# Graph attention and a gated message layer over 8192 nodes: rows renumbered for the mask transposes, four weights made at a block's start

## The chip, the cores and the metric

One NeuronCore of a Trainium2 chip runs the whole program in one launch. The metric is the device time of that launch in microseconds (us), median of the runs shown; the profile is of one further execution, whose own time stands in the table below.

## The reference, cut to what matters

`x` is 8192 x 128 in float32, `adj` is an 8192 x 8192 matrix of zeros and ones in float32 (268 MB), and the layers are two.

```
h  = relu(layernorm(x));  Wh = h @ W;  f1 = Wh @ a1;  f2 = Wh @ a2
e  = leaky_relu(f1 + f2.T, 0.2);  scores = where(adj > 0, e, -9e15)
x1 = x + relu(softmax(scores) @ Wh)
h  = relu(layernorm(x1));  node = h @ W1
y  = einsum('nk,nkf->nf', node, einsum('nc,kcf->nkf', h, W2))
out = x1 + relu(adj @ y + node @ b)
```

The softmax weight of target i and source j is a product of exponentials of f1 and f2 and the mask, so the kernel computes each weight as `max(z_i, q_j) * mask` and sums `weight * (b_j Wh_j)` on TensorE; a 129th column gives the denominator.

## The kernel before, in words

**Numbering.** A block is 1024 nodes: 8 tiles of 128. Node `8p + t` of a block lies on partition `p` in tile `t` (the views in lines 53 to 55). The columns of `adj` go through the same numbering, because four neighbouring columns become four bytes of one 4-byte word, and the transposes work on words.

**Mask.** For each target block `ib` (8 of them) and each source block (8), SyncE loads a 1024 x 1024 piece of `adj` (4 MB) in two loads `h` (L287), one of the tiles 0 to 3 and one of the tiles 4 to 7. Each buffer `q = 2p + h` waits for `adj_cast`, that is, for ScalarE to have cast the piece before. ScalarE casts it to bytes (L507), TensorE transposes it as 32-bit words (`turn_mask`, L757): a chunk is four transposes, one per target tile, and chunk `k` takes the words `k // 2, k // 2 + 2, ...` of the 256 words in a row of 1024 bytes. So the 128 words that one transpose loads as its weights lie two words apart. ScalarE copies a chunk out (`evict`, L519) to `mt`, and stores `mt` to HBM (L626) for the second layer.

**Attention.** The loop is over `ib`, and in it over four `jg` with two half turns `p` each: one half turn is one source block, and has four steps `k`. In a step VectorE makes two weights of 128 x 1024 (`weigh`, L1008) into `p_sb` number `r = 2 * (k % 2) + b_`; TensorE transposes one chunk, then sums each weight into three PSUM banks (L824, 16 matmul instructions per weight), and tells `p_used[r]`. TensorE, in order, starts the sums of a block when ScalarE has copied out the banks of the block before (`copy_sums`, L602).

**Block's end.** While block `ib` is summed, the eight tiles of block `ib - 1` are finished, one per half turn: VectorE in steps 0, 1 and 2 (`finish_tile`: L979; L984, L989, L992, L995; L998, L1001), TensorE turns the result after the first sums of step 2 (L796) and multiplies it by the 16 matrices of `W2` in steps 2 and 3 (L789), ScalarE scales (L585) and GpSimd adds up (`fold`, L389, L392) and stores. Between the blocks, VectorE runs `end_block`: `start_weights` (before: the two weights of step 0 of the next block), then it waits for the sums copied out by ScalarE and computes the denominators (L1057, L1059, L1062). In `turn`, the variable `weighed` says which weights were made ahead. In block 0 nothing is finished, and `scale_rows` scales the value rows in step 1.

**Second layer.** `gather` (L881) multiplies the stored masks with the messages, four blocks' pairs after each other; `store_out` (L662) stores 512 KB for each block of 1024 rows.

**Start.** SyncE loads `x` in eight pieces of 512 KB (L293) between the first loads of `adj`; VectorE takes the statistics of piece `i + 1` (L912, L916) before it norms piece `i` (L927).

Of the kernel before, what the change touches and what calls it, by code (L numbers as in the profile page):

```python
# [38 lines left out]
def build(nc, x, adj, W, a1, a2, W1, W2, b, out):  # L39
    N, D = x.shape  # L40
    K = W1.shape[1]
    P = 128
    T = 8
    BLK = P * T
    NB = N // BLK
# [3 lines left out]
    IT = NB // 2  # L49
    HT = T // 2  # L50
    assert NB == T and BLK == 2 * HB and D == P

    adj_v = adj.rearrange("(i p t) n -> i p t n", p=P, t=T)
    x_v = x.rearrange("(i p t) f -> i p t f", p=P, t=T)
    out_v = out.rearrange("(i p t) f -> i p t f", p=P, t=T)

    zrow_d = nc.dram_tensor("zrow_d", [NT, P], FP32).ap()
    maskT_d = nc.dram_tensor("maskT_d", [NB, NB, P, C * BLK], U16).ap()
# [6 lines left out]
    with ctx:  # L65
# [15 lines left out]
        m8_words = nc.alloc_sbuf_tensor_at("m8_words", [P, 2, T, BLK // 4], FP32, offset=m8_at)  # L81
# [10 lines left out]
        ident = sb("ident", [P, P])  # L92
# [189 lines left out]
        @block.sync  # L282
        def _(sp):

            def load_adj(ib, jg, p, h):
                q = 2 * p + h
                sp.dma_start(adj_sb[:, q, :].rearrange("p (t n) -> p t n", n=BLK),  # L287
                             adj_v[bass.ds(ib, 1), :, h * HT:(h + 1) * HT,
                                   bass.ds((2 * jg + p) * BLK, BLK)].rearrange("i p t n -> (i p) t n"))\
                  .then_inc(adj_in[q], 16)  # L290

            for i in range(NB):
                sp.dma_start(wh[:, i * T:(i + 1) * T, :], x_v[i]).then_inc(x_in[i], 16)  # L293
                if i in (3, 5):
                    load_adj(0, 0, 0, (i - 3) // 2)
            sp.dma_start(wcat[:, 0:K * D].rearrange("c (k f) -> c k f", f=D),
                         W2.rearrange("k c f -> c k f")).then_inc(w2_in, 16)

            def turn(i, ib, jg, finish, last):
                for p in range(2):  # L300
                    for h in range(2):
                        q = 2 * p + h
                        if not (isinstance(i, int) and i == 0 and p == 0):
                            sp.wait_ge(adj_cast[q], i)
                            load_adj(ib, jg, p, h)

            attention_loop(sp, turn)


            for q in range(4):  # L310
                sp.wait_ge(adj_cast[q], NB * IT)
            for p in range(2):
                sp.wait_ge(mt_stored[p], 16 * 2 * IT)

            def load_messages(s):
                o = ORDER[s]
                sp.dma_start(msgs[:, o * T:(o + 1) * T, :, :].rearrange("p n c f -> p (n c f)").bitcast(FP32),
                             msg_d[:, o * T:(o + 1) * T, :].rearrange("p n f -> p (n f)").bitcast(FP32))\
                  .then_inc(msgs_in[s], 16)

            def load_masks(ii, s):
                q = s % 4

                if isinstance(ii, int) and s >= 4:
                    sp.wait_ge(conv_dve, dve_count(True, (s - 3) * T - 1, 1))
                    sp.wait_ge(conv_act, act_count(True, (s - 3) * T - 1, 1))
                elif not isinstance(ii, int):
                    sp.wait_ge(conv_dve, first_dve + (ii - 1) * NT + (s - 3) * T)
                    sp.sem_inc(past_sp, 1)
                    done = act_count(True, (s + 5) * T - 1, 1) if s < 4 else first_act + (s - 3) * T  # L330
                    sp.wait_ge(conv_act, (ii - 1) * NT + done)
                    sp.sem_inc(past_sp, 1)
                sp.dma_start(masks_w[:, q, :, :],
                             maskT_d[ORDER[s], bass.ds(2 * ii, 2), :, :].rearrange("i p w -> p i w"))\
                  .then_inc(masks_in[q], 16)

            def load_kept(ii):
                sp.wait_ge(out_ready, ii * 4 + 4)
                sp.dma_start(keeps[:, :, :], keep_d[:, bass.ds(2 * T * ii, 2 * T), :]).then_inc(keeps_in, 16)

            for s in range(4):
                load_masks(0, s)
            sp.wait_ge(turned, C * NB * NB)
            sp.wait_ge(kept, (ORDER[0] + 1) * T + 2)
            load_messages(0)
            for p in range(2):
                sp.wait_ge(mt_stored[p], 16 * NB * IT)
            for r in range(4):
                sp.wait_ge(p_used[r], 4 * NB * IT)
            for s in range(1, NB - 1):  # L350
                sp.wait_ge(kept, (ORDER[s] + 1) * T + 2)
                load_messages(s)
            for s in range(4, NB):
                load_masks(0, s)
            load_kept(0)
            with sp.Fori(0, NB // 2 - 1) as before:
                for s in range(NB):
                    load_masks(before + 1, s)
                sp.wait_ge(kept, NT + 2)
                load_kept(before + 1)  # L360
# [108 lines left out]
        def _(act):  # L469
# [118 lines left out]

            def load_xt(pb):
                act.wait_ge(mv_done, T * pb + 1)  # L590
                act.dma_start(xt[:, :, :], x_v[bass.ds(pb, 1)].rearrange("i p t f -> (i p) t f")).then_inc(xt_in, 16)

            def copy_sums(ib):
                if not (isinstance(ib, int) and ib == 0):
# [64 lines left out]

            def store_out(ii, h):  # L660
                act.wait_ge(out_ready, 4 * ii + 2 * h + 6)
                act.dma_start(out_v[bass.ds(2 * ii + h, 1)].rearrange("i p t f -> (i p) t f"),  # L662
                              outs[:, h * T:(h + 1) * T, :]).then_inc(out_stored, 16)

            convert(0, True, 1)
            for t in range(NT):
# [32 lines left out]
        def _(pe):  # L699
# [49 lines left out]
            def turn_mask(chunk, k, p, casts):  # L749

                if k < 2:
                    pe.wait_ge(adj_cast[2 * p + k], casts)
                if not (isinstance(chunk, int) and chunk < 2):
                    pe.wait_ge(evicted, chunk - 1)
                words = mt_ps[k % 2][:, :]
                for t in range(HT):
                    ins = pe.transpose(words[:, t * P:(t + 1) * P],  # L757
                                       m8_words[:, p, k % 2 * HT + t, k // 2:BLK // 4:2], ident[:, :])
                ins.then_inc(turned, 1)

            pe.wait_ge(hT_done, 2 * NB)
# [143 lines left out]
        def _(dve):  # L905
# [1 line left out]
            dve.sem_inc(mv_done, 1)  # L907
            dve.sem_inc(out_ready, 4)
            def statistics(i):
                dve.wait_ge(x_in[i], 16)  # L910
                for n in range(T * i, T * (i + 1)):
                    ins = dve.bn_stats(stat8[:, n, :], wh[:, n, :])  # L912
                ins.then_inc(stats8, 1)
                dve.wait_ge(stats8, i + 1)
                for n in range(T * i, T * (i + 1)):
                    ins = dve.bn_aggr(mv8[:, n, :], stat8[:, n, :])  # L916
                ins.then_inc(mv8_done, 1)
# [86 lines left out]
            def weigh(n, i, ib, p, k, b_, tile):  # L1004

                r = 2 * (k % 2) + b_
                dve.wait_ge(p_used[r], 4 * i + 2 * p + k // 2)
                dve.scalar_tensor_tensor(p_sb[:, r, :], zbf[:, bass.ds((ib % 2) * BLK, BLK)],  # L1008
                                         qcol[:, bass.ds(tile + b_, 1)], mtb[:, p, k // 2, :, 2 * (k % 2) + b_],
                                         ALU.max, ALU.mult).then_inc(p_ready, 1)  # L1010

            def turn(i, ib, jg, finish, last):
                for p in range(2):
                    n = 2 * i + p
                    u = i - IT
                    for k in range(C):
                        tile = (2 * jg + p) * T + 2 * k
                        dve.wait_ge(evicted, C * n + 2 * (k // 2) + 2)

                        weighed = p == 0 and k == 0 and isinstance(jg, int) and jg == 0  # L1020
                        if not weighed:
                            weigh(n, i, ib, p, k, 0, tile)
                        if finish and k < 3:
                            finish_tile(k, p, u, 2 * u + p, 2 * jg + p, ib - 1)
                        if not weighed:
                            weigh(n, i, ib, p, k, 1, tile)
                        if not finish and k == 1 and not (ends_block(jg) and p == 1):
                            scale_rows(n + 1)

            def start_weights(ib):  # L1030

                if isinstance(ib, int) and ib == 0:
                    dve.wait_ge(z0_copied, 2)
                else:
                    dve.wait_ge(zb_in, 16 * ib)
                dve.wait_ge(evicted, C * NB * ib + 2)
                for b_ in range(2):
                    weigh(NB * ib, IT * ib, ib, 0, 0, b_, 0)

            def convert(ii, first, t):  # L1040
                s, r = t // T, t % 2
# [95 lines left out]
```

## Time and profile before

| what | value |
|---|---|
| median of 3 runs | 1836.14 us (1834.46 to 1836.53) |
| profiled execution | 1837.21 us, span from first to last instruction 1835.6 us |
| granted TensorE clock, mean | 0.996 |
| TensorE matmul busy | 1807.8 us (98%) |
| weight load busy | 1580.7 us (86%) |
| VectorE busy | 1159.3 us (63%) |
| ScalarE busy | 1328.2 us (72%) |
| GpSimd busy | 634.4 us (35%) |
| DMA | 452.16 MB, mean 246 GB/s |

Busy time of matmuls overlaps, because they are pipelined; what a matmul costs is the distance from its start to the next one's start. "Idle before" is idle time of the engine just ahead of a group of instructions, and behind the arrow stands what ended it.

### The profile page before, as it was taken

How to read it: one execution, taken by the hardware profiler on the slowest of the kernel's cores; microseconds unless marked ns; L12 is line 12 of the kernel's file. 1: busy time of each engine (PE TensorE's matmuls, PEld its weight loads, DVE VectorE, ACT ScalarE, POOL GpSimd, SP SyncE). 2: the span in 40 equal slices, each digit the busy share in tenths (PEclk: the TensorE clock that was granted, in tenths of full speed). 3: DMA queues.
4: the chain of work that ended last, by engine and by line, in shares of the span. 5: the costliest groups of instructions: out<-in, count | busy, mean ns of one | idle time of the engine just before them, and what ended most of it. 6: DMA issues, size and time to landing. Idle time of an engine off the chain costs nothing.

```text
span 1835.6 us, 36204 instructions
## 1 busy us (share of the span) xinstructions
PE 1807.8 (98%) x12320; PEld 1580.7 (86%) x12320; DVE 1159.3 (63%) x1519; ACT 1328.2 (72%) x2145; POOL 634.4 (35%) x522
## 2 busy tenths in 40 slices
PE   8999999999999999999999999999999999999998
PEld 5899989889988988998898889889877788888886
DVE  7666667766766776676667667767665543443434
ACT  6866888788788788887888887788456555555554
POOL 0000255445544554554455445455554400000000
PEclk9999999999999999999999999999999999999999
DMA  9798867776777677678767767772933344445430
GB/s 330 281 354 317 329 254 278 295 290 246 294 296 268 265 299 292 247 285 297 280 252 302 289 260 271 293 288 105 393 127 140 147 161 184 145 182 199 154 143 23
DMA packets 105808, 452.16 MB, mean 246 GB/s; under 512 B 6737, under 2 KB 15137, under 8 KB 87969
## 3 DMA queue, kind: packets, MB, share of 16 engines
q1 hardware_dynamic: 86720, 356.53, 51.9%
q10 hardware_dynamic: 12208, 75.62, 10.1%
q0 software_dynamic: 6832, 19.41, 3.0%
q8 instruction: 27, 0.44, 0.1%
q14 instruction: 21, 0.16, 0.0%
HBM read 364.46 MB, written 87.07 MB: 246 GB/s over the span
## 4 chain that ended last, share of the span: by engine, by line
PE 90%; DVE 4%; ACT 2%; issue 1%; DMA 1%; POOL 0%; DVEq 0%; ACTq 0%; SPq 0%; POOLq 0%
PE ot_ps L824 47%; PE ot_ps L881 12%; PE mt_ps L881 12%; PE hw_ps L789 11%; PE mt_ps L757 6%; PE h_ps L784 1%; DVE p_sb L927 1%; DVE att L984 1%; ACT wh_mask L507 1%; ACT prod L585 1%; DVE p_sb L912 1%; DVE p_sb L1008 0%; DMA wh_mask<-in_x_dram 0%; DVE keep L989 0%; PE h_ps L796 0%
## 5 line engine op out<-in xcount | busy, mean ns | idle before, releaser
L824 PE MATMUL ot_ps<-wh_mask,p_sb 128*128 (+1 forms) x8192 | 964.3, 275 | 7.7 <-DVE p_sb L1008 7.7
L824 PEld LDWEIGHTS ot_ps<-wh_mask,p_sb 128*128 128x128 f32 x8192 | 942.5, 192 | 9.4 <-DVE p_sb L1008 8.9
L1008 DVE SCALAR_TENSOR_TENSOR p_sb<-zb,qcol,mt 128x1024 f32<-128x1024 uint8 (+1 forms) x512 | 730.6, 1455 | 246.6 <-PE ot_ps L824 172.2
L389 POOL TENSOR_TENSOR prod<-prod 128x1024 f32<-128x1024 f32 (+2 forms) x192 | 336.8, 1754 | 571.3 <-ACT prod L585 560.9
L507 ACT ACTIVATE wh_mask<-adj_sb 128x2048 uint8<-128x2048 f32 x256 | 493.5, 1932 | 1.0 <-ACT mt L519 1.0
L612 ACT ACTIVATE mask<-adj_sb 128x1024 fp32r<-128x1024 uint8 x240 | 255.5, 1065 | 173.5 <-PE ot_ps L881 173.4
L1047 DVE CAST mask<-adj_sb 128x1024 fp32r<-128x1024 uint8 x272 | 203.8, 756 | 244.4 <-PE mt_ps L881 242.9
L519 ACT ACTIVATE mt<-mt_ps 128x1024 uint16<-128x1024 uint16 x256 | 267.9, 1047 | 124.8 <-PE mt_ps L757 124.1
L585 ACT ACTIVATE prod<-hw_ps,node 128x128 f32<-128x128 f32 x1024 | 279.1, 387 | 90.8 <-PE hw_ps L789 89.8
L881 PE MATMUL mt_ps<-mask,msgs 128*128 128x512 f32 x1024 | 282.3, 397 | 1.9 <-DVE mask L1047 1.0
L881 PE MATMUL ot_ps<-mask,msgs 128*128 128x512 f32 x1024 | 274.8, 390 | 0.7
L789 PE MATMUL hw_ps<-wcat,hT 128*128 128x512 f32 x512 | 240.7, 592 | 0.0
L881 PEld LDWEIGHTS mt_ps<-mask,msgs 128*128 128x128 f32 x1024 | 191.0, 188 | 51.2 <-issue 13.0
L881 PEld LDWEIGHTS ot_ps<-mask,msgs 128*128 128x128 f32 x1024 | 191.6, 188 | 43.5 <-issue 3.4
L757 PEld LDWEIGHTS mt_ps<-ident,m_words 128*128 128x128 f32 x1024 | 151.1, 204 | 52.7 <-issue 52.3
L757 PE MATMUL mt_ps<-ident,m_words 128*128 128x128 f32 x1024 | 163.1, 282 | 0.3
L789 PEld LDWEIGHTS hw_ps<-wcat,hT 128*128 128x128 f32 x512 | 88.6, 190 | 61.8 <-issue 61.2
L392 POOL TENSOR_TENSOR msg<-prod 128x128 f32<-128x128 f32 x64 | 88.8, 1388 | 5.0
L406 POOL TENSOR_TENSOR msg<-msg 128x128 fp32r<-128x128 f32 x56 | 68.1, 1216 | 4.5
L417 POOL DMA_DIRECT2D zb<-zrow_d x7 | 3.8, 544 | 178.9 <-DVE p_sb L1008 119.8
L404 POOL CAST msg<-msg 128x128 fp32r<-128x128 f32 x56 | 58.9, 1052 | 9.3 <-POOL msg L392 9.3
L575 ACT ACTIVATE node<-h_ps 128x16 f32<-128x16 f32 x64 | 11.9, 186 | 60.0 <-PE h_ps L784 60.0
(110 smaller groups left out, 610.8 us busy)
## 6 DMA issues: line engine op xcount, KB each, us to landing
adj_sb<-in_adj_dram SPq DMA_DIRECT2D x128, 2048.0 KB, 8.7
maskT_d<-mt ACTq DMA_DIRECT2D x64, 1024.0 KB, 5.6
adj_sb<-maskT_d SPq DMA_DIRECT2D x32, 2048.0 KB, 7.7
keep_d<-keep POOLq DMA_DIRECT2D x64, 128.0 KB, 6.1
p_sb<-keep_d SPq DMA_DIRECT2D x4, 2048.0 KB, 12.0
msg_d<-msg POOLq DMA_DIRECT2D x56, 128.0 KB, 6.0
msgs<-msg_d SPq DMA_DIRECT2D x7, 1024.0 KB, 8.9
wh_mask<-in_x_dram SPq DMA_DIRECT2D x8, 512.0 KB, 10.1
```

The lines of the kernel that those rows point to most:

```text
L389: pool.tensor_tensor(prod[:, 0:n, :], prod[:, 0:n, :], prod[:, n:2 * n, :], ALU.add)\
L392: pool.tensor_tensor(msg32[:, :], prod[:, 0, :], prod[:, 1, :], ALU.add).then_inc(prod_read, 1)
L507: ins = act.activation(m8[:, q // 2, t:t + HT // 2, :].rearrange("p t n -> p (t n)"), adj_sb[:, q, part * (HT // 2) * BLK:(part + 1) * (HT ...
L519: act.activation(mt[:, p, k, :], mt_ps[k % 2][:, :].bitcast(U16), ACT.Copy).then_inc(evicted, 1)
L585: ins = act.activation(prod[:, head, :], hw_ps[g % 2][:, j * D:(j + 1) * D], ACT.Copy, scale=node[:, head:head + 1])
L612: act.activation(mask32[:, r, ib, :], masks[:, s % 4, ib, t % T // 4, :, t % 4], ACT.Copy)\
L757: ins = pe.transpose(words[:, t * P:(t + 1) * P], m8_words[:, p, k % 2 * HT + t, k // 2:BLK // 4:2], ident[:, :])
L789: pe.matmul(hw_ps[g % 2][:, :], hT[:, :], wcat[:, g * HB:(g + 1) * HB], start=True, stop=True)\
L824: ins = pe.matmul(ot_ps[h][:, (t - t0) * ROW:(t - t0 + 1) * ROW], p_sb[:, r, t * P:(t + 1) * P], rows, start=begin and t == t0, stop=end a ...
L881: ins = pe.matmul(acc_ps[2 * ib + h][:, :], msgs[:, ORDER[s] * T + t % T, c, :], mask32[:, r, ib, h * HB:(h + 1) * HB], start=t == 0 and c ...
L1008: dve.scalar_tensor_tensor(p_sb[:, r, :], zbf[:, bass.ds((ib % 2) * BLK, BLK)], qcol[:, bass.ds(tile + b_, 1)], mtb[:, p, k // 2, :, 2 * ( ...
L1047: dve.tensor_copy(mask32[:, r, ib, :], masks[:, s % 4, ib, t % T // 4, :, t % 4])\
```

## The change

It has two parts.

Rows and columns are renumbered: node `512h + 4p + b` of a block now lies on partition `p` in tile `4h + b`, in `adj`, `x` and the output alike. A transpose then takes words `128h` to `128h + 127`, one unbroken run. A load of `adj` takes 512 neighbouring rows; it still moves four pieces of 4 KB per partition. A load of `x` is split in two of 256 KB with two counts of its semaphore (16 loads in the place of 8); `xt` and the stores of the output move two pieces of 2 KB per partition instead of one of 4 KB.

VectorE makes the weights of steps 0 and 1 of the next block, four in all, in `start_weights`, before it computes the denominators of the old block. In the first half turn of a block it then makes none in steps 0 and 1.

```
-    adj_v = adj.rearrange("(i p t) n -> i p t n", p=P, t=T)
-    x_v = x.rearrange("(i p t) f -> i p t f", p=P, t=T)
-    out_v = out.rearrange("(i p t) f -> i p t f", p=P, t=T)
+    adj_v = adj.rearrange("(i h p b) n -> i h p b n", h=2, p=P, b=HT)
+    x_v = x.rearrange("(i h p b) f -> i p h (b f)", h=2, p=P, b=HT)
+    out_v = out.rearrange("(i h p b) f -> i p h (b f)", h=2, p=P, b=HT)
...
-                             adj_v[bass.ds(ib, 1), :, h * HT:(h + 1) * HT,
-                                   bass.ds((2 * jg + p) * BLK, BLK)].rearrange("i p t n -> (i p) t n"))\
+                             adj_v[bass.ds(ib, 1), h, :, :, bass.ds((2 * jg + p) * BLK, BLK)]
+                             .rearrange("i p b n -> (i p) b n"))\
...
-                sp.dma_start(wh[:, i * T:(i + 1) * T, :], x_v[i]).then_inc(x_in[i], 16)
+                for h in range(2):
+                    sp.dma_start(wh[:, i * T + h * HT:i * T + (h + 1) * HT, :],
+                                 x_v[i, :, h, :].rearrange("p (b f) -> p b f", f=D)).then_inc(x_in[i], 16)
...
-                act.dma_start(xt[:, :, :], x_v[bass.ds(pb, 1)].rearrange("i p t f -> (i p) t f")).then_inc(xt_in, 16)
+                act.dma_start(xt[:, :, :].rearrange("p (h b) f -> p h (b f)", h=2), x_v[bass.ds(pb, 1)].rearrange("i p h g -> (i p) h g")).then_inc(xt_in, 16)
...
-                act.dma_start(out_v[bass.ds(2 * ii + h, 1)].rearrange("i p t f -> (i p) t f"),
-                              outs[:, h * T:(h + 1) * T, :]).then_inc(out_stored, 16)
+                act.dma_start(out_v[bass.ds(2 * ii + h, 1)].rearrange("i p h g -> (i p) h g"),
+                              outs[:, h * T:(h + 1) * T, :].rearrange("p (h b) f -> p h (b f)", h=2)).then_inc(out_stored, 16)
...
-                                       m8_words[:, p, k % 2 * HT + t, k // 2:BLK // 4:2], ident[:, :])
+                                       m8_words[:, p, k % 2 * HT + t, (k // 2) * P:(k // 2 + 1) * P], ident[:, :])
...
-                dve.wait_ge(x_in[i], 16)
+                dve.wait_ge(x_in[i], 32)
...
-                        weighed = p == 0 and k == 0 and isinstance(jg, int) and jg == 0
+                        weighed = p == 0 and k < 2 and isinstance(jg, int) and jg == 0
...
-                for b_ in range(2):
-                    weigh(NB * ib, IT * ib, ib, 0, 0, b_, 0)
+                for k in range(2):
+                    for b_ in range(2):
+                        weigh(NB * ib, IT * ib, ib, 0, k, b_, 2 * k)
```

## Rows read from the trace of the kernel before

**Rows 1.** Busy time of each engine in the stretch of the attention.
```profile
core 0: us, PE busy (x) PEld busy (x) DVE busy (x) ACT busy (x) POOL busy (x), PEclk, DMA share, GB/s
52.00:1316.00 1264.00, 1254.15 (x9834) 1144.12 (x9835) 873.74 (x948) 996.09 (x1655) 561.66 (x447) 1.00 0.74 281
```

**Rows 2.** Waits of the whole trace: who for whom, us, times, longest.
```profile
PE ot_ps L824 <- DVE p_sb L1008: 7.7, 6, 1.4
```

**Rows 3.** Groups by line and shape: busy us, mean ns of one, idle before.
```profile
L757 PE MATMUL mt_ps<-ident,m_words 128*128 128x128 f32 x1024 | 163.1, 282 | 0.3
L757 PEld LDWEIGHTS mt_ps<-ident,m_words 128*128 128x128 f32 x1024 | 151.1, 204 | 52.7 <-issue 52.3 <-ACT wh_mask L507 0.3
L796 PEld LDWEIGHTS h_ps<-ident,xn 128*128 128x128 f32 x64 | 9.1, 143 | 1.2 <-DVE xn L1001 0.9
```

**Rows 4.** Timeline, chunks of four transposes and what follows: start us, us, what.
```profile
506.53 0.63 PE L757 MATMUL mt_ps<-ident,m_words 128*128 128x128 f32 x4
507.00 3.74 PE L824 MATMUL ot_ps<-wh_mask,p_sb 128*128 128x129 f32 x32
...
516.33 0.64 PE L757 MATMUL mt_ps<-ident,m_words 128*128 128x128 f32 x4
516.81 1.95 PE L824 MATMUL ot_ps<-wh_mask,p_sb 128*128 128x129 f32 x16
...
1827.29 0.60 PE L853 MATMUL ot_ps<-ident,prod 128*128 128x128 f32 x4
1827.72 0.60 PE L853 MATMUL h_ps<-ident,prod 128*128 128x128 f32 x4
```

**Rows 5.** Timeline of all engines, the boundary of two blocks at 510 us.
```profile
503.18 2.87 DVE L1008 SCALAR_TENSOR_TENSOR p_sb<-zb,qcol,mt 128x1024 f32<-128x1024 uint8 x2
...
511.84 0.17 DVE L1057 TENSOR_SCALAR empty<-ut 128x8 f32<-128x8 f32 x1 [5.78 <-ACT ut L602]
...
512.89 0.35 DVE L979 SCALAR_TENSOR_TENSOR att<-whsum,empty,ut 128x128 f32<-128x128 f32 x1 [0.44 <-DVE rden L1062]
513.21 1.28 DVE L1008 SCALAR_TENSOR_TENSOR p_sb<-zb,qcol,mt 128x1024 f32<-128x1024 uint8 x1
...
514.03 4.84 POOL L389 TENSOR_TENSOR prod<-prod 128x1024 f32<-128x1024 f32 x3 [8.49 <-ACT prod L585]
514.41 2.39 DVE L984 TENSOR_SCALAR att<-att,rden 128x128 f32<-128x128 f32 x1
...
517.00 1.22 DVE L989 TENSOR_TENSOR keep<-att,xt 128x128 f32<-128x128 f32 x1 [0.19 <-DVE att L984]
...
518.79 2.65 DVE L1008 SCALAR_TENSOR_TENSOR p_sb<-zb,qcol,mt 128x1024 f32<-128x1024 uint8 x2
...
520.09 2.05 PE L824 MATMUL ot_ps<-wh_mask,p_sb 128*128 128x129 f32 x16 [1.33 <-DVE p_sb L1008]
```

**Rows 6.** The same view, the first boundary, where GpSimd has nothing to fold.
```profile
193.96 0.28 DVE L984 TENSOR_SCALAR att<-att,rden 128x128 f32<-128x128 f32 x1
194.43 0.29 DVE L989 TENSOR_TENSOR keep<-att,xt 128x128 f32<-128x128 f32 x1 [0.19 <-DVE att L984]
...
195.62 3.74 PE L824 MATMUL ot_ps<-wh_mask,p_sb 128*128 128x129 f32 x32
```

**Rows 7.** Chain of waits at the start: start us, us, what.
```profile
0.99 0.69 SPq L293
...
1.74 8.03 DMA wh_mask<-in_x_dram
```

**Rows 8.** DMA issues: count, KB each, us from issue to landing.
```profile
adj_sb<-in_adj_dram SPq DMA_DIRECT2D x128, 2048.0 KB, 8.7
xt<-in_x_dram ACTq DMA_DIRECT2D x8, 512.0 KB, 7.1
```

**Rows 9.** Timeline, one load of `adj` and the first cast of it.
```profile
404.22 0.37 SPq L287 DMA_DIRECT2D adj_sb<-in_adj_dram  x1
...
438.38 1.90 ACT L507 ACTIVATE wh_mask<-adj_sb 128x2048 uint8<-128x2048 f32 x1
```

## The prediction

> **What bounds the kernel now.** I read the stretches first. Of the 1264 us of the attention (blocks 0 to 7) TensorE has a matmul under way for 1254.15 us, ScalarE is busy for 996.09, VectorE for 873.74, and the DMA engines for 0.74 of the time, at a granted clock of 1.00 [rows 1]. So TensorE sets the pace there, and what its instruction stream loses is time. Then the waits, for what it waits on in that stretch: only VectorE's weights, 7.7 us in 6 times [rows 2]. Six of the seven boundaries between blocks have such a wait, and nothing else in the stretch stops TensorE for as long. The rest can only fall if its own instructions come closer together, so the third view is that of the groups by shape, and the fourth the timeline, where the distance from start to start is the price. The second layer is not touched but for its stores.
>
> **Part 1, the transposes.** There are 1024 of them in 256 chunks of four. Their weight load, which reads words two apart, takes 204 ns; that of the other float32 transposes, which reads 128 words in a run, takes 143 ns (L796) [rows 3]. The load overlaps the matmul before it, so this difference is not the gain. The gain is in the distances. Behind sums, four transposes take 516.81 - 516.33 = 0.48 us to the start of the next sums, and behind a 512 column matmul 507.00 - 506.53 = 0.47 us [rows 4]. Four transposes of unbroken words take 1827.72 - 1827.29 = 0.43 us by the same reckoning [rows 4]; and from the spans, (0.64 - 0.28) / 3 = 0.12 us each against (0.60 - 0.27) / 3 = 0.11, where 0.28 and 0.27 are the lengths of one. Two decimals leave 0.03 to 0.05 us a chunk. I take 0.037, the lower half, because the first distance of a chunk behind a long matmul has its weight load hidden already. 256 x 0.037 = 9.5 us, between 256 x 0.03 = 7.7 and 256 x 0.05 = 12.8; below, a mechanism that isn't stride gives 0. All chunks but the first few lie in TensorE's unbroken stream, so all of it reaches the end. What is late next is nothing: ScalarE has 0.79 of the stretch and the DMA engines 0.74, and the stretch shrinks by under 1.5%.
>
> The Trainium skill speaks against this part. The page Advanced Engine Details and Errata, section SBUF Cachelines, says that reads keep full rate as long as two of them fall on each line of 16 bytes. Float32 words two apart do just that, so by this rule the stride is free, the transposes gain nothing, and the sum below would be 9.5 us higher; it is rival C. The trace disagrees as far as it can: 204 ns against 143.
>
> **Part 2, four weights ahead.** What happens at a boundary now: TensorE ends the old sums at 507.00 + 3.74 = 510.74 [rows 4]; VectorE has made two new weights (503.18 to 506.05) and idles 5.78 us until ScalarE has copied the sums, at 511.84 [rows 5]. Then come the denominators, the first step of finishing, the third weight at 513.21, and behind it L984, which takes 2.39 us, and L989, which takes 1.22. At the first boundary, where GpSimd folds nothing, these take 0.28 and 0.29 and TensorE goes on without a gap [rows 6]. At this one GpSimd's fold starts at 514.03, and VectorE's two end just behind the ends of its additions [rows 5]. So the fourth weight is made from 518.79, and TensorE, which could have started at about 516.81 + 16 x 0.112 = 518.60 (0.112 us from sum to sum: 3.74 less the last one's length of 0.28, over 31), starts at 520.09. That is 1.49 us, and the sums behind it take 2.05 instead of 1.95, 0.10 more [rows 4, 5]. Over six boundaries: 7.7 us of idle, and 6 x (0.16 + 0.10), since the idle is counted from the end of the last matmul, 0.16 behind the point at which the next could start: 9.3 us.
>
> After: the third weight needs the sums of buffer 2, done about 1.9 us before 510.74, the fourth those of buffer 3 at 510.74. A weight takes 1.28 us, so the third lies in idle time and the fourth ends at about 512.08. Both are there long before 516.8. The denominators wait behind the fourth and come 0.24 us later than now, the first finishing step the same, and L984 comes at about 513.7 to 513.8, because no weight lies between. That is just ahead of GpSimd's 514.03. If VectorE is first, the finishing is done by about 515. If L984 falls behind GpSimd, it ends at 516.8 and L989 at 518.2, as now, and the mean and variance at 518.8; but then the first weight of step 2 follows at once and is done at 520.1. TensorE wants it at 516.81 + 3.6 + 0.5 = 520.9 (two weights' sums, one chunk). What could be late next is the second weight of step 2: behind L998 and L1001, wanted at 522.7. With L1001 held once more by GpSimd's L392 or by the cast behind it, to 521.6, that weight comes at about 523.1, 0.4 us late. I take 0.2 us for all six together, 9.1 us gained; the bounds are 9.3 and 9.3 - 6 x 0.8 = 4.5. The first boundary gives nothing, and in block 0 the order of VectorE's work does not change: the same four weights come first either way.
>
> The wait for `p_used[3]` in `start_weights` now stands ahead of the denominators. What is queued behind it are L1057 to L1062 and the finishing; ScalarE's copies end at 511.84 anyway, 1.1 us behind that release, so only the 0.24 us counts. The loads of `zb` by GpSimd wait on weights that come no later. Without its idle time as cover, this step would cost VectorE 2.56 us a block, at six blocks 15 us.
>
> **Part 3, loads and stores of the new rows.** *adj*: 2 MB in pieces of 4 KB as before, 8.7 us to landing [rows 8]; the load issued at 404.22 is cast from 438.38 on [rows 9], so 25 us of slack hide any small difference. *x at the start*: the chain begins with the second piece, issued behind 0.69 us of the first and 8.03 us in landing [rows 7]; from there on VectorE works without a pause. Four issues now stand where two stood. No row has a 256 KB piece of 512-byte runs; at 0.69 us for double the runs, and 0.37 us for an issue with few descriptors (L287) [rows 9], I put one at about 0.5, so the second piece is all issued 4 x 0.5 - 2 x 0.7 = 0.6 us later. Bounds: 2 x 0.69 = 1.4 us on top, and 0.5 below nothing, if halves in flight land earlier. I take +0.4. The six later pieces have slack. *xt*: 7.1 us to landing [rows 8], issued some 12 us before its use; hidden. *Stores*: only the last one is bare; 16 pieces per engine instead of 8, the same bytes; +0.1 us, bounds 0 and 0.5.
>
> **Sum.** -9.5 - 9.1 + 0.4 + 0.1 = -18.1 us. Against the profiled execution, 1837.21 (span 1835.6 and 1.6 around it), that is 1819.1; the median of the runs is 1.07 lower, 1836.14, so 1818.0 is the forecast for a median. What can be told from no change here is about 0.2%, 3.7 us.
>
> **Rivals.**
> A, the forecast: both parts work, 1818.
> B, the wait moves: L984, L989 and L1001 each fall behind a GpSimd addition, and the second weight of step 2 is late by 0.4 to 0.8 us at six boundaries: 2.4 to 4.8 us less gain, 1820 to 1823. For it: the times are close (513.8 against 514.03). Against: 0.8 us of margin at the weight before.
> C, the stride is free and the 204 ns are due to something else, such as ScalarE writing the same buffer: 1818.0 + 9.5 = 1827.5. Against it: not only the load is longer, but the distance too, in the chunk at 506.53 as in that at 516.33 [rows 4].
> D, slower: `adj` comes slower. The same 4 KB pieces now lie 128 KB apart from partition to partition instead of 256 KB, and if memory serves that badly, the loads become the bound. The DMA engines are busy for 0.74 of the stretch, so it decides from 1 / 0.74 = 1.35 times the present time per piece (8.7 us becoming 11.7), less what the gain takes off. At 1.5 times, 1264 x 0.74 x 1.5 = 1403 us in the place of 1264: +139, 1975 us; at 1.4 times, +45, 1881. For it speaks only that no row shows this order; against it, pieces and bytes are the same.
> E, the change does nothing at boundaries, because the fourth weight's wait for the last sums holds VectorE until ScalarE's copy anyway and the stall goes elsewhere in full: 1818.0 + 9.1 = 1827.1. Against it: 2.56 us of weights move from behind the stall into idle time.
>
> **Chances.** A 0.72, B 0.11, C 0.07, E 0.04, D 0.03, and 0.03 for slower or level by something unseen. The range goes from 1813 (12.8 - 9.5 more from the transposes, 0.5 + 0.4 less at the start, and a microsecond between executions) to 1826: that holds A and B with the bounds of the start and stores, and leaves out C, D, E. Faster by over 0.2% is A, B, C, E: 0.94, of which I take 0.02 off for mishaps that no case names; within 0.2% 0.03; slower 0.05, D and the unseen.
>
> **What would show it.** Weight loads of L757 at about 140 ns and chunks of 0.44 us; no wait of TensorE for L1008, four weights running between 503 and 512 of that boundary, denominators 0.2 us behind the copied sums, L984 short or at least no stall behind it; landing of `adj` still near 8.7 us; the first norm of the start at most 1.4 us later. Wrong would be: L757 at 204 ns (C), a new wait of L824 for L1008 in step 2 (B), casts of ScalarE waiting for `adj` (D).

## The result and the profile after

The changed kernel takes 1817.96 us (median, 1816.49 to 1818.7, 4 runs) against 1835.52 (1834.46 to 1836.53) for the kernel before: a ratio of 0.990, 95% interval 0.9888 to 0.9911, 17.6 us less. The forecast was 1818.0 in a range of 1813 to 1826. The profiled execution took 1816.49 us, span 1814.9.

Lines from about 300 on have numbers two or three higher in the changed kernel: the transposes are L759, the sums L826, the weights L1010, the finishing L981, L986, L991, L1003, the fold L391, the second layer L883.

The stretches, from the starts of the first and last sums, of the kernel before and of the changed one (number, shortest/median/longest in ns, first to last start in us):

```profile
L824 PE MATMUL ot_ps<-wh_mask,p_sb x8192: 272/275/378, 61.1 to 1315.6; 128*128 x147, 128*128 128x129 f32 x53
L881 PE MATMUL ot_ps<-mask,msgs x1024: 387/389/472, 1318.4 to 1825.2; 128*128 128x512 f32 x171
```

```profile
L826 PE MATMUL ot_ps<-wh_mask,p_sb x8192: 272/275/377, 57.8 to 1294.3; 128*128 x147, 128*128 128x129 f32 x53
L883 PE MATMUL ot_ps<-mask,msgs x1024: 387/389/473, 1297.1 to 1804.3; 128*128 128x512 f32 x171
```

The attention went from 1254.5 to 1236.5 us, 18.0 less; the second layer stayed (506.8 and 507.2); the start is 3.3 us shorter, of which below. Of the two executions' difference of 20.7 us, the 18.0 are where the two parts work, and the start belongs to the execution, as shown below.

Groups by line and shape, the changed kernel, which answer to [rows 3], and the wait that answers to [rows 2]:

```profile
L759 PE MATMUL mt_ps<-ident,m_words 128*128 128x128 f32 x1024 | 153.4, 273 | 0.4 <-ACT mt L521 0.2 <-ACT wh_mask L509 0.2
L759 PEld LDWEIGHTS mt_ps<-ident,m_words 128*128 128x128 f32 x1024 | 123.6, 141 | 58.7 <-issue 58.3 <-ACT wh_mask L509 0.4
...
PE ot_ps L826 <- DVE p_sb L1010: 0.8, 1, 0.8
```

The weight load of a transpose fell from 204 to 141 ns, and TensorE's six waits for weights are gone; the one of 0.8 us that is left is that of the very first sums. The boundary at 510 us of [rows 5] is now at 502 us. Timeline of VectorE, TensorE and GpSimd there:

```profile
500.78 1.28 DVE L1010 SCALAR_TENSOR_TENSOR p_sb<-zb,qcol,mt 128x1024 f32<-128x1024 uint8 x1 [2.90 <-PE ot_ps L826]
502.57 1.28 DVE L1010 SCALAR_TENSOR_TENSOR p_sb<-zb,qcol,mt 128x1024 f32<-128x1024 uint8 x1 [0.50 <-PE ot_ps L826]
503.77 0.16 DVE L1060 TENSOR_SCALAR empty<-ut 128x8 f32<-128x8 f32 x1
...
505.21 0.29 DVE L986 TENSOR_SCALAR att<-att,rden 128x128 f32<-128x128 f32 x1
505.69 0.29 DVE L991 TENSOR_TENSOR keep<-att,xt 128x128 f32<-128x128 f32 x1 [0.20 <-DVE att L986]
...
506.90 2.40 DVE L1010 SCALAR_TENSOR_TENSOR p_sb<-zb,qcol,mt 128x1024 f32<-128x1024 uint8 x1 [0.25 <-ACT mt L521]
510.12 0.16 DVE L1000 RECIPROCAL rstd<-std 128x1 f32<-128x1 f32 x1 [0.83 <-ACT std L569]
...
498.79 3.74 PE L826 MATMUL ot_ps<-wh_mask,p_sb 128*128 128x129 f32 x32
...
504.52 3.74 PE L826 MATMUL ot_ps<-wh_mask,p_sb 128*128 128x129 f32 x32
508.09 0.60 PE L759 MATMUL mt_ps<-ident,m_words 128*128 128x128 f32 x4
508.53 3.74 PE L826 MATMUL ot_ps<-wh_mask,p_sb 128*128 128x129 f32 x32
512.11 0.60 PE L759 MATMUL mt_ps<-ident,m_words 128*128 128x128 f32 x4
512.54 1.95 PE L826 MATMUL ot_ps<-wh_mask,p_sb 128*128 128x129 f32 x16
...
505.83 5.42 POOL L391 TENSOR_TENSOR prod<-prod 128x1024 f32<-128x1024 f32 x3 [8.43 <-ACT prod L587]
```

The third and fourth weights lie in what was VectorE's idle time, each as soon as its buffer is free. L986 and L991 come at 505.21 and 505.69, just ahead of the fold's start at 505.83, and take 0.29 us each in the place of 2.39 and 1.22 [rows 5]. What the fold holds now is the first weight of step 2 (2.40 us in the place of 1.28), done at 509.30, 3.2 us before TensorE wants it at 512.54. TensorE has no gap, and a chunk takes 508.53 - 508.09 = 0.44 us.

### The profile page after: what moved, and what is told of

Its sections match the earlier page's. It is cut to its first block, busy times and chain, and to the rows that moved or that the text cites. A ratio compares the mean times of both kernels' runs of the same rounds, so it can differ in the third digit from the quotient of the medians.

```text
span 1814.9 us, 36206 instructions
## 1 busy us (share of the span) xinstructions
PE 1793.4 (99%) x12320; PEld 1563.8 (86%) x12320; DVE 1181.3 (65%) x1519; ACT 1326.1 (73%) x2145; POOL 667.5 (37%) x522
## 4 chain that ended last, share of the span: by engine, by line
PE 95%; DVE 3%; ACT 1%; issue 1%; DMA 0%; POOL 0%; SPq 0%; ACTq 0%; POOLq 0%; DVEq 0%
PE ot_ps L826 50%; PE ot_ps L883 13%; PE mt_ps L883 12%; PE hw_ps L791 12%; PE mt_ps L759 6%; PE h_ps L786 1%; DVE p_sb L929 1%; DVE p_sb L914 1%; PE h_ps L798 0%; POOL prod L391 0%; DVE mask L1050 0%; PE ot_ps L734 0%; DVE p_sb L918 0%; DMA wh_mask<-in_x_dram 0%; ACT wh_mask L509 0%
## 5 line engine op out<-in xcount | busy, mean ns | idle before, releaser
L826 PE MATMUL ot_ps<-wh_mask,p_sb 128*128 (+1 forms) x8192 | 962.8, 275 | 0.8 <-DVE p_sb L1010 0.8
L826 PEld LDWEIGHTS ot_ps<-wh_mask,p_sb 128*128 128x128 f32 x8192 | 939.3, 192 | 1.5 <-DVE p_sb L1010 1.0
L1010 DVE SCALAR_TENSOR_TENSOR p_sb<-zb,qcol,mt 128x1024 f32<-128x1024 uint8 (+1 forms) x512 | 775.1, 1544 | 210.2 <-PE ot_ps L826 178.3
L391 POOL TENSOR_TENSOR prod<-prod 128x1024 f32<-128x1024 f32 (+2 forms) x192 | 367.7, 1915 | 521.5 <-ACT prod L587 503.8
L883 PE MATMUL mt_ps<-mask,msgs 128*128 128x512 f32 x1024 | 282.6, 398 | 1.9 <-DVE mask L1050 1.0
L883 PE MATMUL ot_ps<-mask,msgs 128*128 128x512 f32 x1024 | 274.8, 390 | 1.1 <-DVE mask L1050 0.5
L883 PEld LDWEIGHTS mt_ps<-mask,msgs 128*128 128x128 f32 x1024 | 191.2, 188 | 51.1 <-issue 13.0
L883 PEld LDWEIGHTS ot_ps<-mask,msgs 128*128 128x128 f32 x1024 | 191.8, 188 | 43.6 <-issue 3.8
L759 PEld LDWEIGHTS mt_ps<-ident,m_words 128*128 128x128 f32 x1024 | 123.6, 141 | 58.7 <-issue 58.3
L759 PE MATMUL mt_ps<-ident,m_words 128*128 128x128 f32 x1024 | 153.4, 273 | 0.4 <-ACT mt L521 0.2
L791 PEld LDWEIGHTS hw_ps<-wcat,hT 128*128 128x128 f32 x512 | 88.8, 191 | 61.7 <-issue 61.1
L991 DVE TENSOR_TENSOR keep<-att,xt 128x128 f32<-128x128 f32 x64 | 18.7, 292 | 99.0 <-POOLq L385 92.9
L408 POOL TENSOR_TENSOR msg<-msg 128x128 fp32r<-128x128 f32 x56 | 72.7, 1298 | 4.5
```

Source lines behind the costliest of these rows:

```text
L391: pool.tensor_tensor(prod[:, 0:n, :], prod[:, 0:n, :], prod[:, n:2 * n, :], ALU.add)\
L759: ins = pe.transpose(words[:, t * P:(t + 1) * P], m8_words[:, p, k % 2 * HT + t, (k // 2) * P:(k // 2 + 1) * P], ident[:, :])
L791: pe.matmul(hw_ps[g % 2][:, :], hT[:, :], wcat[:, g * HB:(g + 1) * HB], start=True, stop=True)\
L826: ins = pe.matmul(ot_ps[h][:, (t - t0) * ROW:(t - t0 + 1) * ROW], p_sb[:, r, t * P:(t + 1) * P], rows, start=begin and t == t0, stop=end a ...
L883: ins = pe.matmul(acc_ps[2 * ib + h][:, :], msgs[:, ORDER[s] * T + t % T, c, :], mask32[:, r, ib, h * HB:(h + 1) * HB], start=t == 0 and c ...
```

## The experiments

All times are medians; "attention" is from the first to the last start of the sums, as above, in one profiled execution. It is the sharper measure: 1236.50 us in both executions of the changed kernel that were profiled, while the first sums began at 57.7 to 61.1 us over all fourteen traces.

**The parts, one at a time.** First the renumbering alone:

```
-                for k in range(2):
-                    for b_ in range(2):
-                        weigh(NB * ib, IT * ib, ib, 0, k, b_, 2 * k)
+                for b_ in range(2):
+                    weigh(NB * ib, IT * ib, ib, 0, 0, b_, 0)
```

> The changed kernel with two weights made ahead instead of four: the renumbering alone, with the split loads of x. Theory (two independent gains: unbroken words 9.5 us, four weights 9.1 us): weight loads of the transposes at about 141 ns, about 0.109 us from transpose to transpose, six waits of TensorE for VectorE's weights of about 1.3 us left, and 9 to 11 us less than the kernel before, a ratio of 0.994 to 0.995. Rival (the gains overlap: closer transposes make VectorE late, or the waits close up by themselves): the six waits change by more than 1 us in sum, and the ratio is under 0.993 or over 0.997.

1826.24 us, ratio 0.9949 (0.9935 to 0.9962). The attention is 1246.4, 8.1 less than before. TensorE waits for weights 9.0 us in 7 times, longest 1.5; without the first sums' 0.8 that is 0.5 more than the 7.7 of before: where the transposes are closer, TensorE comes earlier to the fourth weight, which is not earlier itself. The six waits changed by less than 1 us in sum, so the rival is out.

Then the four weights alone, `weighed` and `start_weights` of the changed kernel in the one before:

> The kernel before with four weights made ahead and nothing else. Theory: no wait of TensorE for a weight at a block boundary, transposes as before (204 ns weight loads), 9 us less, a ratio of 0.995. Rival (the wait moves to the second weight of step 2): waits of 0.4 to 0.8 us at six boundaries in step 2, 4.5 to 7 us less, a ratio of 0.996 to 0.9975.

1825.77 us, ratio 0.9945 (0.9931 to 0.9958). The attention is 1245.3, 9.2 less, and no wait at a boundary is left. The rival is out, and so is rival E of the prediction, by which the stall would only have moved.

Then the stride without the renumbering:

```
-                                       m8_words[:, p, k % 2 * HT + t, k // 2:BLK // 4:2], ident[:, :])
+                                       m8_words[:, p, k % 2 * HT + t, (k // 2) * P:(k // 2 + 1) * P], ident[:, :])
```

> The kernel before, but each transpose takes 128 unbroken words while rows and columns keep their old numbering, so the mask is applied to the wrong sources: it isolates the stride from every change of a load. Theory (the stride of the weight load alone): weight loads at 141 ns, 0.037 us less per chunk, 9.5 us in all, and the start as before. Rival (part of the gain of the renumbering comes from the loads, through the start or through adj): less than 8 us here, or a start that is over 1 us from that of the kernel before.

1827.78 us, ratio 0.9955 (0.9941 to 0.9969), attention 1246.4: the same as with the whole renumbering, so the loads of the new numbering give and cost nothing there. The weight load is 141 ns. The 8.1 us are less than the theory's 9.5 and sit at the edge of its rival's 8.

And the changed kernel beside them:

> The changed kernel once more beside the others: 17.5 to 18.5 us under the kernel before, and the sum of the gains of the renumbering alone and of the four weights alone within 1.5 us of it.

1817.36 us, 18.7 less than the 1836.07 of the kernel before, 0.2 over what was expected; ratio 0.9898 (0.9883 to 0.9913). In the attention the parts give 8.1 + 9.2 = 17.3 us and both together 18.0: once the boundary waits are gone, the transposes give 1245.3 - 1236.5 = 8.8. By the medians the parts give 9.8 and 10.3 us, 20.1 in sum, 1.4 over both together: within what was expected, and a sign of how little medians of four or five runs resolve.

**The start.**

```
-                sp.dma_start(wh[:, i * T:(i + 1) * T, :], x_v[i]).then_inc(x_in[i], 16)
+                for h in range(2):
+                    sp.dma_start(wh[:, i * T + h * HT:i * T + (h + 1) * HT, :],
+                                 x_v[i, :, h * HT:(h + 1) * HT, :]).then_inc(x_in[i], 16)
```

> The kernel before, with each load of x at the start split into two of four tiles, old numbering. Theory from the trace of the changed kernel (the split itself brings the second piece of x earlier, because more loads are in flight): the first norm starts 1 to 1.5 us earlier than in the kernel before, and so do the first sums. Rival (the 2 KB runs of the new numbering do it, or chance of one execution): the first norm within 0.5 us of the kernel before, or later by up to 1.4 us as first forecast.

1835.85 us, ratio 1.0001 (0.9992 to 1.001). The first norm starts at 11.1 us; in the kernel before it was 12.23, in the changed one 10.9. But the five other kernels that load `x` unsplit have it at 11.0 to 11.2 (11.16 on average), and the other split ones at 10.8 to 11.0 (10.89 for all eight). So the 1.4 us were almost all chance of the one execution shown ahead of the prediction, whose second piece landed late (8.03 us in [rows 7]); by these averages the split brings about 0.3 us, and no time of a run shows it. The rest of the shorter start is TensorE's clock. Timeline of TensorE, the product of the diagonals, before and after:

```profile
55.21 3.78 PE L772 MATMUL hw_ps<-prod,ones 128*128 128x512 f32 x4 [1.26 <-DVE prod L961]
```

```profile
53.85 1.98 PE L774 MATMUL hw_ps<-prod,ones 128*128 128x512 f32 x4 [1.26 <-DVE prod L963]
```

The same four instructions take 3.78 us in one execution and 1.98 in the other; the mean granted clock from 45 to 70 us was 0.86 and 1.00; in the kernel before it was 0.50 from 57 to 60 us, that is, 1.2 in the place of 2.4 GHz. TensorE had idled the same 1.26 us just before in both executions, so what decided is not shown. The second execution of the changed kernel has 0.93 over that stretch, its first sums at 59.3 us: the slow piece belongs to the execution and not to the kernel.

**What makes the fourth weight late.** Only its place, with two weights still made ahead:

```
+                        early = finish and p == 0 and k == 1 and isinstance(jg, int) and jg == 0
+                        if early:
+                            weigh(n, i, ib, p, k, 1, tile)
                         if finish and k < 3:
                             finish_tile(k, p, u, 2 * u + p, 2 * jg + p, ib - 1)
-                        if not weighed:
+                        if not weighed and not early:
```

> The kernel before, two weights ahead, but in the first half turn of a block VectorE makes the fourth weight ahead of the finishing of step 1. Theory (what makes TensorE wait is the fourth weight's place behind L984 and L989, which are held by GpSimd's fold, not how many weights are ahead): the six waits are gone, about 9 us less, as with four ahead. Rival (VectorE is short of time at the boundary and needs its idle time for weights): a wait stays, less than 6 us gained.

1832.61 us, ratio 0.9986 (0.9977 to 0.9995), attention 1251.8: 2.7 us gained, not 9. TensorE still waits for weights, 5.5 us in 7 times. My theory fell. VectorE, GpSimd and TensorE at the same boundary:

```profile
510.50 4.59 DVE L1008 SCALAR_TENSOR_TENSOR p_sb<-zb,qcol,mt 128x1024 f32<-128x1024 uint8 x2
511.31 5.71 POOL L389 TENSOR_TENSOR prod<-prod 128x1024 f32<-128x1024 f32 x3 [8.48 <-ACT prod L585]
515.01 1.29 DVE L984 TENSOR_SCALAR att<-att,rden 128x128 f32<-128x128 f32 x1
...
517.84 1.28 DVE L1008 SCALAR_TENSOR_TENSOR p_sb<-zb,qcol,mt 128x1024 f32<-128x1024 uint8 x1
...
514.10 3.74 PE L824 MATMUL ot_ps<-wh_mask,p_sb 128*128 128x129 f32 x32
519.18 2.05 PE L824 MATMUL ot_ps<-wh_mask,p_sb 128*128 128x129 f32 x16 [0.87 <-DVE p_sb L1008]
```

The third and fourth weight take 4.59 us, where two unhindered ones take 2 x 1.28: the fourth is itself held by the fold (from 511.31 on), the finishing then comes behind it, and TensorE, which now gets its fourth weight in time, waits in step 2 instead, 0.87 us. That is what rival B of the prediction feared, a wait that moves to step 2, but at the first weight of the step, where B had it at the second.

Three weights ahead:

```
+                weigh(NB * ib, IT * ib, ib, 0, 1, 0, 2)
```

> The kernel before with three weights ahead: the fourth still stands behind L984 and L989. Theory: without the third weight ahead of it L984 comes at about 513.3 to 513.4 of that boundary, before GpSimd's fold at 514.0, L989 at 513.8, so neither is held and the fourth weight is ready by about 516: no wait, 9 us less. Rival (L989 loses the race with the fold): the fourth weight ends at about 518.5 to 520 against 518.6 wanted, and 0 to 1.5 us per boundary stay, 0 to 9 us gained.

1826.72 us, ratio 0.9949 (0.9936 to 0.9963), attention 1245.4, as with four. L984 comes 0.74 us and L989 0.26 us ahead of the fold:

```profile
511.17 0.29 DVE L984 TENSOR_SCALAR att<-att,rden 128x128 f32<-128x128 f32 x1
511.65 0.29 DVE L989 TENSOR_TENSOR keep<-att,xt 128x128 f32<-128x128 f32 x1 [0.20 <-DVE att L984]
...
512.71 4.84 DVE L1008 SCALAR_TENSOR_TENSOR p_sb<-zb,qcol,mt 128x1024 f32<-128x1024 uint8 x2
...
511.91 6.23 POOL L389 TENSOR_TENSOR prod<-prod 128x1024 f32<-128x1024 f32 x3 [6.87 <-ACT prod L585]
```

What matters is that the weight that stood between the denominators and L984 is out of the way. The two weights behind them are held by the fold (4.84 us in the place of 2 x 1.28), but both are there before TensorE wants them. The fourth ahead adds nothing.

The fold itself, taken away from the kernel before:

```
-                    pool.tensor_tensor(prod[:, 0:n, :], prod[:, 0:n, :], prod[:, n:2 * n, :], ALU.add)\
+                    pool.tensor_tensor(prod[:, 0:1, 0:16], prod[:, 0:1, 0:16], prod[:, n:n + 1, 0:16], ALU.add)\
```

> The kernel before, but GpSimd's three folding additions (L389) take 16 elements each instead of 1024, 512 and 256 columns, so the messages are not summed: it takes GpSimd's long additions away and nothing else. Theory (VectorE's L984 and L989 are held at the boundary by GpSimd's additions): L984 0.28 and L989 0.29 us at the boundaries instead of 2.39 and 1.22, no wait of TensorE there, 9.2 us less with two weights ahead; the mean length of a weight falls from 1455 ns towards 1280. Rival (VectorE is simply late there, whoever runs beside it): the six waits stay, under 3 us less.

1820.55 us, ratio 0.9921 (0.9908 to 0.9935). TensorE no longer waits for a weight at a boundary. The attention is 1245.3, to 0.1 us what four and three weights ahead gave, with two ahead and in the old order:

```profile
508.84 1.28 DVE L1008 SCALAR_TENSOR_TENSOR p_sb<-zb,qcol,mt 128x1024 f32<-128x1024 uint8 x1
510.04 0.28 DVE L984 TENSOR_SCALAR att<-att,rden 128x128 f32<-128x128 f32 x1
510.51 0.29 DVE L989 TENSOR_TENSOR keep<-att,xt 128x128 f32<-128x128 f32 x1 [0.19 <-DVE att L984]
```

So GpSimd's additions hold VectorE, and they are the whole of the six waits.

The Trainium skill has this rule (SBUF — State Buffer, section Who interferes with whom): VectorE shares one pair of ports with GpSimd, needs it for two inputs in SBUF and in its two-port modes, and who comes second waits for the whole instruction. The trace agrees with the waiting: 2.39 against 0.28 us for L984, which has one input in SBUF, and 1.22 against 0.29 us for L989, which has two, both 128 x 128. That it is a matter of ports no run here shows.

**The stride.** Words four apart:

```
-                                       m8_words[:, p, k % 2 * HT + t, (k // 2) * P:(k // 2 + 1) * P], ident[:, :])
+                                       m8_words[:, p, (k % 2 * HT + t) // 2 * 2:(k % 2 * HT + t) // 2 * 2 + 2, :].rearrange("p r n -> p (r n)")[:, k // 2:2 * BLK // 4:4], ident[:, :])
```

> The changed kernel, but each transpose takes words four apart out of two rows, so the mask is applied to the wrong sources and targets. With two apart a transpose cost 0.118 us and its weight load 204 ns, unbroken 0.109 us and 141 ns. Theory (the weight load is paced by the 16-byte lines or so that it touches, and shows once it is longer than the stream of 128 float32 columns): with four apart each word is on a line of its own, the weight load grows by another 50 to 110 ns, and a transpose costs 0.15 to 0.24 us, 10 to 30 us more than unbroken. Rival (any break costs the same fixed piece): 204 ns and 0.118 us again, 9.5 us more than unbroken.

1827.81 us, attention 1246.0: 9.5 us over the changed kernel, where 10 to 30 were expected of the theory. The weight load did not grow by another 50 to 110 ns but by 2 (208 against 206, medians), and the attention is 0.7 us over that of words two apart with four weights ahead (1245.3). The theory of lines fell and the rival held.

Unbroken words from an odd word on, and words eight apart:

```
+                                       m8_words[:, p, k % 2 * HT + t, 1 + (k // 2) * (P - 2):1 + (k // 2) * (P - 2) + P], ident[:, :])
```

> The changed kernel, each transpose taking 128 unbroken words from an odd word on (1 and 127), so the mask is applied to the wrong sources. If the fast load needs two neighbouring words of one aligned 8 bytes, it costs like words two apart: 208 ns and 0.118 us each, 9 us more in the attention. If it only needs a step of one word: 141 ns and 0.109 us, the attention at 1236.5 us as in the changed kernel. I hold the second for likelier.

```
+                                       m8_words[:, p, k % 2 * HT:k % 2 * HT + HT, :].rearrange("p r n -> p (r n)")[:, k // 2 + 2 * (t % 4):HT * BLK // 4:8], ident[:, :])
```

> The changed kernel, each transpose taking words eight apart out of four rows, so the mask is applied to the wrong sources and targets. Words four apart cost as much as two apart. Theory (any step but one puts the load in one slower way of reading, whatever lines it touches): 208 ns and 0.118 us once more, 9.5 us over the changed kernel. Rival (the cost grows with the distance, from eight on): over 0.13 us each, 12 us or more on top of that.

The odd start costs nothing: 1817.54 us, attention 1236.5. Eight apart gave 1819.45 us and an attention of 1237.8, only 1.3 us more than unbroken, and neither of the expectations. The weight loads of four apart, eight apart and the odd start (shortest/median/longest ns):

```profile
L759 PEld LDWEIGHTS mt_ps<-ident,m_words x1024: 194/208/221, 48.9 to 1287.5; 128*128 128x128 f32 x171
```

```profile
L759 PEld LDWEIGHTS mt_ps<-ident,m_words x1024: 185/188/230, 48.9 to 1280.5; 128*128 128x128 f32 x171
```

```profile
L759 PEld LDWEIGHTS mt_ps<-ident,m_words x1024: 138/141/145, 48.7 to 1277.8; 128*128 128x128 f32 x171
```

So 188 ns cost 1.3 us in the attention, 206 and 208 ns cost 8.8 and 9.5. Where between them the cost sets in was not measured. It is not simply where the load is longer than the time to the next start, because even the 141 ns are longer than the 109 ns of that. Why eight apart is quicker than four is open.

**A version that beats both.** Without the fold the second layer was shorter too, by 5.3 us. In its first pass VectorE has extra conversions in steps 1 and 4 of each seven, and the fold runs beside steps 0 to 2. VectorE and GpSimd there, in the changed kernel:

```profile
1331.19 1.36 DVE L1003 TENSOR_SCALAR xn<-keep,mv,rstd 128x128 f32<-128x128 f32 x1
1332.47 4.39 DVE L1050 CAST mask<-adj_sb 128x1024 fp32r<-128x1024 uint8 x4
...
1329.98 5.46 POOL L391 TENSOR_TENSOR prod<-prod 128x1024 f32<-128x1024 f32 x3 [9.76 <-ACT prod L587]
```

A conversion takes 0.69 us (median), four of them 4.39 beside the fold.

```
-            return ib == 0 or (first and t < T * PERIOD and t % PERIOD in (1, 4))
+            return ib == 0 or (first and t < T * PERIOD and t % PERIOD in (4, 5))
```

> The changed kernel with VectorE's extra conversions of the second layer's first pass moved from steps 1 and 4 of each seven to steps 4 and 5. Leaving GpSimd's fold out took 5.3 us off the second layer (507.84 to 502.52 us), beside what it did in the attention. Theory (there too the fold holds VectorE, whose conversions in steps 1 and 2 then come late by about 0.5 us in each of eight periods): with one conversion fewer beside the fold, 2 to 5 us less in the second layer, the attention unchanged at 1236.5, a ratio to the kernel before of 0.9872 to 0.9888. Rival (ScalarE, which takes that conversion, is late instead): the second layer within 1 us of 508.4, ratio 0.990, or longer.

1814.05 us (1813.47 to 1814.54), ratio 0.988 (0.9864 to 0.9897) to the kernel before. The second layer, first to last start:

```profile
L883 PE MATMUL ot_ps<-mask,msgs x1024: 387/389/400, 1297.6 to 1801.4; 128*128 128x512 f32 x171
```

503.8 us in the place of 507.2, the attention as it was (1236.4). From one start of L798 to the next, once in seven steps, the traces have 17.0 to 17.1 us in the changed kernel (once 17.5), 16.6 here and 16.6 without the fold (L796 there), the first seven steps left out. So the shift gives back what the fold cost in each seven steps, though the fold still holds the conversions beside it. The theory held, and ScalarE was not late instead.

## Why the prediction was right

The mechanism of both parts was right. That the time was forecast to 0.1 us is luck: the terms were off by up to 0.7 us, and medians of the kernel before lie between 1835.52 and 1836.79 us, those of the changed one at 1817.96 and 1817.36. The forecast was reckoned from 1836.14; from the 1835.52 of the result it would have been 1817.4. The change itself was forecast as 18.1 us and measured as 17.6 and 18.7.

- *The bound.* TensorE's stream sets the attention: what was taken out of it came off the time, and nothing else became late. VectorE rose to 899 us busy in 1249 (one of its weights takes 1544 ns on average, 1455 before, and 1301 in the kernel before without the fold), ScalarE stayed at 998, the DMA share was 0.75.
- *Transposes, 9.5 us forecast.* 8.8 us beside the four weights, 8.1 alone. The mechanism was right: the gain is in the distances from start to start, not in the length of the load. The size was read from two decimals of a timeline. To the nanosecond, the four distances of a chunk were 115, 120, 120 and 120 ns behind sums and 109, 117, 120 and 120 behind a 512 column matmul (medians of the trace of before), and are 109 each now. That is 38 and 29 ns a chunk, where 37 was taken for all; the first distance gains less, as the prediction said. Alone, half a microsecond is given back at the boundaries, which the prediction did not see.
- *The rule of 16-byte lines (rival C)*, which the prediction takes from the Trainium skill (Advanced Engine Details and Errata, section SBUF Cachelines), would have given no gain. Measured: 63 ns of load and 8.8 us. The run with unbroken words and the old numbering has the load at 141 ns too, so it was not ScalarE's writing of the same buffer either. And words eight apart, each on a line of its own, are quicker than two apart with two on a line, so the line is not what counts here.
- *Boundaries, 9.1 us forecast.* 9.2. The order of events came as written, with L986 2.7 us behind the end of the old sums where 3.0 was forecast, and ahead of the fold. What I did not see is that the weights themselves are held by the fold, in the changed kernel by 1.1 us at this boundary (2.40 in the place of 1.28); the 3.2 us of margin in step 2 hid it. That margin, 0.8 us in the forecast, is also what put rival B out. The reading that the fourth weight must be ahead was too strong: three do.
- *Start, +0.4 us.* Wrong in sign and too small to matter: 0 to 0.3 less. Four pieces took 6.01 us to issue in halves and 5.80 whole, 0.2 more, where the prediction took 0.6 more for two pieces. The chain of [rows 7] was that of an unusual execution.
- *Stores, +0.1 us.* From the last start of L883 to the end of the span 10.6 us, from that of L881 10.4 before: 0.2 in one pair of executions.
- *Loads of adj (rival D).* 9.1 us to landing in the place of 8.7, and no wait of ScalarE or TensorE for them. Not foreseen: the new order also makes the issue of a load longer on SyncE's queue, 0.54 us in the place of 0.37 (medians), which nothing waits for either.

## What to carry to other kernels

When two small operations of VectorE take four to eight times their length at one place of a loop and not at another, look for what GpSimd runs beside them: in the attention, moving a single weight out from in front of them was worth as much as removing GpSimd's work. Read what straightening a strided weight load would give from start to start, not from its length: 63 ns (means) of load were worth about 9 ns a transpose here. And take a chain at the very start of a program from more than one execution before pricing changes to it.

## What was not expected of the hardware

- The time of a float32 weight load for a transpose does not grow steadily with the distance of its words: 141 ns at one, 206 at two, 208 at four, 188 at eight (medians). The distance from transpose to transpose is about 0.109, 0.118, 0.119 and 0.111 us, by the starts in the traces.
- A weight, which has two inputs in SBUF, can be held by an addition of GpSimd for longer than it takes itself. All 512 weights (shortest/median/longest ns), in the kernel before and without the fold:

```profile
L1008 DVE SCALAR_TENSOR_TENSOR p_sb<-zb,qcol,mt x512: 1252/1285/3355, 59.7 to 1309.4; 128x1024 f32<-128x1024 uint8 x128, 128x1024 f32<-128x1024 f32 x43
```

```profile
L1008 DVE SCALAR_TENSOR_TENSOR p_sb<-zb,qcol,mt x512: 1250/1284/1572, 56.9 to 1294.7; 128x1024 f32<-128x1024 uint8 x128, 128x1024 f32<-128x1024 f32 x43
```

The longest took 3.36 us with the fold and 1.57 without; the median is the same.
